# Pair attention: values projected per tile of 111 tokens, biased into a staging buffer and moved to each image's rows by DMA

## The reference

```
qkv = x @ w_attn + b_attn                     # x: 32 images x 37 tokens x 256
q, k, v = split(qkv)                          # 16 heads of 16 each
att = softmax(where(causal, q @ k.T / 4, -inf))
y = (att @ v) @ w_proj + b_proj
```

## Time and profile before

| | us |
|---|---|
| median of three executions | 1091.79 |
| the profiled execution | 1088.44 |
| its span, first to last instruction | 1086.6 |
| TensorE busy with matmuls | 905.5 (83%) |
| VectorE busy | 607.6 (56%) |
| ScalarE busy | 527.9 (49%) |
| GpSimd busy | 330.2 (30%) |
| mean granted TensorE clock | 0.898 of full |
| data moved by DMA | 47.40 MB |

### The profile page before, as it was taken

One profiled execution on the slowest core, in us unless ns is written; L12 is line 12 of the kernel. 1 busy time (PEld: TensorE's weight loads), 2 busy tenths in 40 slices (PEclk: granted clock), 3 DMA queues, 4 the chain that ended last, 5 costly groups with the idle time before them and its releaser, 6 DMA issues. The chain is left out here.

```text
span 1086.6 us, 26178 instructions
## 1 busy us (share of the span) xinstructions
PE 905.5 (83%) x10336; PEld 671.7 (62%) x10336; DVE 607.6 (56%) x1308; ACT 527.9 (49%) x942; POOL 330.2 (30%) x425
## 2 busy tenths in 40 slices
PE   6889959499999789768997299999478898998666
PEld 6778726377777557557886144444267777777424
DVE  5475656766666279754663624222554564533476
ACT  3345547566566289634452155554123333443346
POOL 1211320445553000020313324442254453532102
PEclk9999968799999899869997599999788999998885
DMA  6200030200000100001012953222220000000001
GB/s 224 83 3 2 3 117 6 82 1 3 0 0 1 45 3 1 0 8 44 20 35 77 407 173 54 42 47 48 65 86 3 2 2 2 2 3 3 1 1 45
DMA packets 24307, 47.40 MB, mean 44 GB/s; under 512 B 4720, under 2 KB 15974, under 8 KB 23555
## 3 DMA queue, kind: packets, MB, share of 16 engines
q1 hardware_dynamic: 19859, 39.09, 10.4%
q0 software_dynamic: 4336, 6.74, 3.3%
HBM read 38.35 MB, written 7.47 MB: 42 GB/s over the span
## 5 line engine op out<-in xcount | busy, mean ns | idle before, releaser
L2755 PE MATMUL psum<-L2f_EW,weights_even 128*64 x176 | 81.7, 608 | 0.5 <-ACT weights_even L2454 0.2
L2756 PE MATMUL psum<-L2f_W,weights_even 128*64 128x512 f32 x176 | 81.7, 608 | 0.0
L2415 POOL DMA_INDIRECT expert_sums<-weights_even,L2f_target x20 | 35.0, 1750 | 76.1 <-DVE weights_even L2637 56.5
L1063 PE MATMUL psum<-L_cT,weights_odd 128*128 128x222 f32 (+1 forms) x192 | 45.1, 365 | 13.2 <-DVE L_by_sin L950 11.8
L2650 DVE TENSOR_TENSOR weights_even<-psum,weights_even 128x512 f32<-128x512 f32 x22 | 15.2, 692 | 72.2 <-PE psum L2756 70.2
L2274 PE MATMUL psum<-weights_even,L1f_H 128*111 128x256 f32 x176 | 46.8, 425 | 7.5 <-DVE L1f_H L2205 7.5
L425 ACT ACTIVATE L_PT<-psum 101x296 f32<-101x296 f32 x64 | 27.0, 421 | 49.1 <-PE psum L621 49.0
L882 ACT ACTIVATE L_U<-psum 128x592 f32<-128x592 f32 x32 | 21.2, 663 | 60.4 <-PE psum L1114 60.4
L2755 PEld LDWEIGHTS psum<-L2f_EW,weights_even 128*64 128x64 f32 x176 | 22.7, 139 | 43.2 <-issue 43.2
L2462 ACT ACTIVATE L2f_W<-L2f_EW 128x1024 f32 x44 | 46.3, 1053 | 6.2 <-PE psum L2756 5.6
L366 POOL TENSOR_TENSOR L_rs<-L_mv,ln_eps 111x2 f32<-111x2 f32 (+1 forms) x12 | 3.0, 252 | 146.0 <-DVE L_mv L518 139.3
(11 more groups left out here) (462 smaller groups left out, 2621.6 us busy)
## 6 DMA issues: line engine op xcount, KB each, us to landing
L2f_EW<-experts SPq DMA_DIRECT2D x24, 512.0 KB, 13.6
weights_even<-L_w SPq DMA_DIRECT2D x4, 1024.0 KB
patch_ring<-patches SPq DMA_DIRECT2D x11, 333.0 KB, 4.7
expert_sums<-L_blank SPq DMA_DIRECT2D x1, 1184.0 KB
weights_odd<-L_wo SPq DMA_DIRECT2D x1, 1024.0 KB
expert_rows<-X SPq DMA_DIRECT2D x5, 192.0 KB
expert_sums<-X SPq DMA_DIRECT2D x5, 192.0 KB
weights_even<-tok_w SPq DMA_DIRECT2D x3, 256.0 KB, 2.9
```

What stands on the lines that cost most here:

```text
L1063: mm = nc.tensor.matmul(bank[:, h * NC2:h * NC2 + width(u)], wu[:, (2 * g + h) * 128:(2 * g + h + 1) * 128], cT[:, u % 2, n // 4, 0:width( ...
L2755: nc.tensor.matmul(core.bank(bank)[PAIR[0], :], xsT[:, j % 2, c, PAIR[0]], own, start=c == 0, stop=c == KD - 1)
L2756: mm = nc.tensor.matmul(core.bank(bank)[PAIR[1], :], xsT[:, j % 2, c, PAIR[1]], cols(W1[:, part], KD, NF)[:, c], start=c == 0, stop=c == K ...
```

## The change

Values are projected like any other dense product, one tile of 111 tokens at a time, with all 256 columns as the moving side: two matmuls a tile, four a unit, both tiles in bank M1. VectorE adds the bias for each tile into a new staging tile `by_tile`, whose rows are still the tile's (three images below one another), and whose ones are filled once. SyncE then moves each image's 37 rows to rows 0 to 36 (parity 0) and 64 to 100 (parity 1) of V: six transfers a unit, each 37 rows with one piece of 544 bytes (8 heads of 16 numbers and a one) for each of the unit's two tiles. `values` waits for these transfers in place of VectorE's addition. V has the parities apart now (2 x 8 x 17 columns for 8 x 34), so the sums come out beside each head. In L2 the copy of the blank is issued behind the first unit's transfers, and each unit's row copies behind the transfers of a later unit.

```diff
-        V = sb("V", [128, 2, IMGS, 8, 34])
+        V = sb("V", [128, 2, IMGS, 2, 8 * 17])
+        by_tile = sb("by_tile", [128, 2, 2, 2, 8 * 17])
...
+        def moves(units):
+            return 16 * sum(2 * min(PER, len(UNITS[u][2])) for u in range(units))
+
+        def rows_of(u):
+            return R if len(UNITS[u][1]) == 2 else width(u)
...
             def _(sp):
                 load_next(sp, next_loads, next_sem)
+                def move_values(u):
+                    images, n = UNITS[u][2], len(UNITS[u][1])
+                    sp.wait_ge(v_done, u + 1)
+                    after(sp, o_ps, pairs_of(u - 1))
+                    for i in range(min(PER, len(images))):
+                        for e in range(2):
+                            sp.dma_start(V[64 * e:64 * e + T, u % 2].rearrange("p (m i) e c -> p m i e c", m=2)[:, 0:n, i, e],
+                                         by_tile[i * T:(i + 1) * T, u % 2, 0:n, e]).then_inc(v_moved, 16)
...
+                sp.wait_ge(zeroed, 2)
+                move_values(0)
                 if route:
                     sp.wait_ge(blank_set, 1)
                     sp.dma_start(core.dram["expert_sums"][SUMS:SUMS + B * T, :].rearrange("(p n) d -> p n d", p=2 * T),
                                  blank[:2 * T].unsqueeze(1).broadcast_to([2 * T, B // 2, D])).then_inc(blank_out, 16)
...
+                for u in range(1, NU):
+                    move_values(u)
+                    if route and u >= 2:
+                        copy_rows(u - 2)
+                if route:
+                    copy_rows(NU - 2)
                     sp.wait_ge(blank_out, 16)
...
+                nc.gpsimd.memset(V[:], 0.0).then_inc(zeroed, 1)
...
-                nc.gpsimd.memset(V[:], 0.0)
-                pool.drain()
-                for e in range(2):
-                    last = nc.gpsimd.memset(V[64 * e:64 * e + T, :, :, :, 32 + e:33 + e], 1.0)
-                last.then_inc(zeroed, 1)
...
+                nc.vector.memset(by_tile[:], 1.0)
+                dve.drain()
...
+                def v_out(u):
+                    n, rows = len(UNITS[u][1]), rows_of(u)
+                    dve.wait_ge(v_ps, u + 1)
+                    after(dve, v_moved, moves(u - 1))
+                    for m in range(n):
+                        last = nc.vector.tensor_tensor(by_tile[:rows, u % 2, m].rearrange("p e (c d) -> p e c d", d=17)[:, :, :, 0:16],
+                                                       core.bank(M1)[:rows, m * D:(m + 1) * D].rearrange("p (e c d) -> p e c d", e=2, c=8),
+                                                       bv[:rows].rearrange("p (e c d) -> p e c d", e=2, c=8), ALU.add)
                     last.then_inc(v_done, 1)
...
+                def v_project(u):
+                    rows = rows_of(u)
+                    after(pe, k_done, u + 1 if u else 0)
+                    for m in range(len(UNITS[u][1])):
                         for kd in range(KD):
-                            for e in range(2):
-                                mm = nc.tensor.matmul(bank[64 * e:64 * e + T, i * 128:(i + 1) * 128], xT[:, u % 2, kd, at(img):at(img) + T],
-                                                      wqkv[:, kd, 2 * D + 128 * e:2 * D + 128 * (e + 1)], start=kd == 0, stop=kd == KD - 1)
+                            mm = nc.tensor.matmul(core.bank(M1)[:rows, m * D:(m + 1) * D], xT[:, u % 2, kd, m * R:m * R + rows],
+                                                  wqkv[:, kd, 2 * D:3 * D], start=kd == 0, stop=kd == KD - 1)
                     mm.then_inc(v_ps, 1)
...
                 def values(s):
                     u = s // 3
-                    pe.wait_ge(v_done, v_phases(u + 1))
+                    pe.wait_ge(v_moved, moves(u + 1))
...
-                                                      PT[:PR, s % 2, cq, b * T:(b + 1) * T], V[:PR, u % 2, (2 * s + b) % IMGS, cq, :],
+                                                      PT[:PR, s % 2, cq, b * T:(b + 1) * T],
+                                                      V[:PR, u % 2, (2 * s + b) % IMGS, :, 17 * cq:17 * (cq + 1)],
...
-                    if s == 0:
-                        v_project(0, 1)
...
-                            v_project(u + 1, 0)
+                            v_project(u + 1)
...
-                    if u + 1 < NU and s % 3 == 2 and images_of(u + 1, 1):
-                        v_project(u + 1, 1)
```

More of the change, by code:

```diff
@@ L249 @@
 PR = 64 + T
[L252 to L260, removed]
 def pairs_of(units):
@@ L390, in x_T @@
                     act.wait_ge(xT_ps, u + 1)
-                    after(act, v_ps, v_phases(u - 1))
+                    after(act, v_ps, u - 1)
                     tiles = UNITS[u][1]
@@ L491, in normalise @@
                     nc.vector.tensor_tensor(O[:PR, s % 2].rearrange("p c (e d) -> p c e d", e=2),
-                                            o[:, :, 0:32].rearrange("p c (e d) -> p c e d", e=2),
+                                            o[:, :, :, 0:16],
                                             r.unsqueeze(3).broadcast_to([PR, 8, 2, 16]), ALU.mult).then_inc(o_done, 1)
[L495 to L499, removed]
-                    for e in range(2):
[L501 to L504, removed]
+                def v_out(u):
[6 more added lines that the diff above has]
+                                                       bv[:rows].rearrange("p (e c d) -> p e c d", e=2, c=8), ALU.add)
                     last.then_inc(v_done, 1)
@@ L559, in x_T @@
                 def x_T(u):
-                    after(pe, v_done, v_phases(u, 0))
+                    after(pe, v_done, u)
                     for m, t in enumerate(UNITS[u][1]):
@@ L576, in q_project @@
                     pe.wait_ge(xT_done, u + 1)
-                    after(pe, v_done, v_phases(u))
+                    after(pe, z_done, u - 2)
                     project(u, core.bank(M2), 0, q_ps)
@@ L678, in _ @@
                 k_project(0)
-                v_project(0, 0)
-                pe.wait_ge(zeroed, 2)
+                v_project(0)
+                pe.wait_ge(zeroed, 1)
                 pe.wait_ge(set_up, 3)
@@ L3117, in layouts @@
         out[f"{n}_bqk"] = column(g[bqkv][:2 * D])
-        out[f"{n}_bv"] = np.zeros((PR, 128), np.float32)
-        for e in range(2):
-            out[f"{n}_bv"][64 * e:64 * e + T] = g[bqkv][order][2 * D + 128 * e:2 * D + 128 * (e + 1)]
+        out[f"{n}_bv"] = row(g[bqkv][order][2 * D:])
         out[f"{n}_wo"], out[f"{n}_bo"] = kmajor(wo[by_pair], KD), row(g[bo])
```

40 lines of the change are left out of this document (16 added, 24 removed).

## The result

| | before | after |
|---|---|---|
| time, median of four executions, us | 1092.48 (1082.33 to 1097.85) | 1158.49 (1149.35 to 1163.54) |
| profiled execution, us | 1088.44 | 1163.54 |
| its span, us | 1086.6 | 1161.7 |
| its mean TensorE clock, of full | 0.898 | 0.869 |
| L0's attention, us | 110.5 | 135.2 |

The account below looks back on a forecast made before the run. TensorE was taken as the bound (100.2 of 110.5 us in L2). L0's 9.6 and L2's 26.2 us plus 6 for the clock, 42 on 1088.4, gave 1131 with some distance to the median; range 1105 to 1168, its own 1118 to 1147.

Parts of the forecast that it names:

- The transfer: Six moves a unit on one DMA engine at 22 GB/s: 13.0 us from the last addition to L634's release.
- +1.6 a unit: Ordinary units of L0 and L2: the moves don't fit into 10.75 us, so the period becomes 18.05 us against 16.47.
- The clock: TensorE's slower clock after ten waits in L0 and L2: 6 us taken, with bounds of nothing and 17.
- The first units: First unit of each stage, with less room for the moves: third step's mask matmul later by 3.2 us (L0), 3.6 (L2).
- The blank: L2's second unit: its moves queue behind the blank copy of about 25 us; +21.4 us, containing the first unit's 3.6.
- TensorE's gain: Values phase in L0 and L2, one wider pass instead of two: net gain 0.7 us a unit, nothing in the last.
- the first rival: Moves of both stages spread over engines or faster, leaving only TensorE's gain and about 1.5 us a stage: 1080, chance 0.08.
- The edits costed at nothing: Both stages: fewer VectorE additions, staging and GpSimd fills, strides of 17 in L634 and the normalisation: zero each.
- The rival in which the blank doesn't hold the moves up: L2's second unit: transfers interleave or the first engine isn't shared, 16.2 us less, 1115 in all; chance 0.12.
- Moves spread over engines: Moves of both stages on two engines or more, fitting into the 10.75 us: 8 to 9 us gained, 1080; chance 0.08.
- Pieces at 14 GB/s: Moves between SBUF rows at the rate of 148 byte pieces: 6.3 us more in each of ten units, 1194; chance 0.10.

Follow-up runs that it names:

- run 1: The changed kernel with each 37-row move cut into transfers of 32 and 5 rows: 1114.06 us, ratio 1.0138 to the kernel before.
- run 11: The changed kernel with surplus matmuls in TensorE's waits for the moves, their numbers fitted to the waits: 1142.06 us, ratio 1.045 to the kernel before.
- Runs 11 and 12: Run 11 and, in the same group as yardstick, the changed kernel itself without an edit: 1142.06 and 1156.5 us, ratios 1.045 and 1.0578.
- Run 2: The changed kernel with the blank copied to DRAM from 32 rows instead of 74, same bytes and place in the queue: 1147.33 us, ratio 1.046.
- run 6: The changed kernel with L2's blank issued ahead of the first moves instead of behind them: 1164.16 us, ratio 1.0604 to the kernel before.
- run 4: The changed kernel with only 68 of the 544 bytes of each piece moved, same number of transfers and pieces: 1100.38 us, ratio 1.001.
- run 3: The changed kernel without the transfers, V filled with ones and L634 waiting for the addition alone: 1079.6 us, ratio 0.9829 to the kernel before.
- both repairs: The changed kernel with moves cut into 32 and 5 rows and the blank copied from 32 rows: 1093.98 us, ratio 0.9939 to the kernel before.

## Why the prediction was right in kind and short in size

**The transfer.** Its mechanism held in all points: one engine (share 0.06 to 0.07), 22 GB/s in its middle, and the new waits at L634. That 37 rows go to one engine follows from the rule of the Trainium skill ("DMA: Bandwidth & Descriptors", section on why a DMA increments its semaphore by 16), and run 1 agrees: cut into 32 rows and 5 rows, the same data show a share of 0.14 and let L635 run without a wait in five of the seven ordinary units. Its duration was mis-sized: 13.0 us was the term, and from the end of the additions (605.3) to the release (619.8) it is 14.5. What was too small is the data time. The rate reached the 22 GB/s taken only later: 14 and 11 GB/s in the first 2 us here, and 13 to 17 GB/s for 6 us in L0's chain that is issued from 115.71 on. In L0's chain from 93.89 on, the data move from about 95.2 to 107.8, 12.6 us for the 11.0 forecast, with 1.3 us ahead and 0.5 behind. An issue took 1.5 us and not 0.3 to 0.8, still less than the data of a move. At full clock (run 11) this alone gives units of 19.1 to 19.3 us, where the forecast had 18.05.

**The ordinary units.** The step that failed is "+1.6 a unit". Measured from third mask matmul to third mask matmul are +4.5, +2.8, +5.9 and +6.4 in L0 and +5.9, +4.7 and +6.25 in L2: 36.45 us for the 11.2 forecast. By run 11 about 20.4 of them stay at full clock (10.6 in L0 and 9.7 in L2), 9 us more than forecast, mostly the 1.5 us of each of seven transfers. 1.3 of the 9 are no fault of the transfer: the seven units took 114.0 us before, not 7 times 16.47 (the last one of each stage 15.3 and 15.1, one in L0 17.8).

**The clock.** The other 16 us are the second failed term: 6 was taken, with bounds of 0 and 17. The short waits were said to cost "a little", and they cost most. The reason is the order: a wait ends, the clock stays low behind it (0.50 for 5.5 us in the unit shown), and into this stretch falls the next unit's values pass, 3.00 us for 1.9. With it the addition and the next transfer start late, and since the transfer ends the unit, every us is passed on to the end. The units of L0 show it: behind values passes of 2.46 and 2.72 us they took 20.64 and 20.99 us, behind 3.15 and 3.64 us 21.70 and 22.34. From the unit's mask matmul to the end of its additions it was 5.94 us, against the 4.35 of the forecast. Runs 11 and 12 put 14.4 us (7 to 21) on it in the time of the kernel. The forecast's reason for a small number, that a slow stretch falls in part into the next wait, is wrong here: in the unit shown the stretch begins about 1 us before the end of its own wait and is over before the next transfer is issued, so none of it falls into the next wait. The ten waits and the 0.58 behind a gap were in the forecast; what they delay was not.

**The first units.** +5.2 us in L0 and +5.7 in L2, from the values pass to the third mask matmul, against 3.2 and 3.6. The 1.5 us of the transfer explain most of it; L634 behind the 8.4 us wait took 1.23 us for 0.77, at the slow clock, and the rest is small.

**The blank.** Forecast 21.4 - 3.6 = 17.8 us on L2's second unit, measured 36.20 - 17.95 = 18.25. Run 2 took it away, run 6 moved it to the first unit, and in run 4 it alone remained. The rival in which the blank doesn't hold the moves up is out.

**TensorE's gain.** 0.7 us a unit forecast, 0.8 measured (runs 1 and 3); and a gain of 2.0 and 1.6 us at the stages' starts (run 3) that the sum had only in the first rival (1.5 a stage). The edits costed at nothing (VectorE, the fills, the strides of 17) show no cost: the addition takes 0.41 to 0.43 us as forecast, and without the transfers both stages are shorter than before.

Added up: 10.9 (first units) + 18.25 (second unit) + 36.45 = 65.6 of the 66.0 us that the two stages grew. The forecast had 6.8 + 17.8 + 11.2 and 6 for the clock, 41.8. That 1158 still lies inside the range of 8 in 10 owes something to luck: its upper part was there for slower pieces, and it was filled by the clock and the first us of each chain. The forecast's own range ended at 1147.

**The rivals.** Moves spread over engines: false for the kernel as it is; run 3, which shows what it would be worth at best, came to 13.2 us less in the two stages, more than the rival's 8 to 9. Pieces at 14 GB/s: true only at the start of a chain (2 to 6 us), false for the rest. The time, 1158, lies between the forecast and this last rival, and it got there another way.

## What to carry to other kernels

Before a transfer is put on a path, factor its row count: 37 rows went over one engine at 22 GB/s, and as 32 + 5 rows the same bytes took 50.7 us less in the two stages; look also for other transfers with few engines on the same queue, since they stand in line on the same one. Where a wait of TensorE comes just ahead of work that starts the next transfer, price the slow clock in full in each period (here 2 us of each 21), because what it delays is the next wait's end. And price a saving together with what it needs: 0.8 us of TensorE a unit was bought with a 14.5 us transfer in a gap of 10.75, and with both repairs 0.6% is left of what the rest of the change is worth without transfers (1.7%, interval 0.9 to 2.5).

## What the hardware showed that was not expected

- A chain of moves from SBUF to SBUF over one engine ran slower at its start (14 and 11 GB/s in the first 2 us of one, 13 to 17 GB/s for 6 us in another) and at 22 GB/s later, with the engine's share the same.
- An issue on SyncE took 1.5 us where the moves go over one engine (six in 9.3 us), 0.75 where they are split (12 in 9.0 us), and 0.67 over one engine with an eighth of the bytes (six in 4.03 us).
- Moves from GpSimd's queue used about three engines at a time but carried 32 GB/s in all, with 1.35 us of GpSimd for each issue.
- Behind waits of TensorE of 3 to 5 us, one in each 21 us, the clock is granted at 0.50 (from about 597 to 603.7 us around the wait that ends at 598.22); three surplus matmuls in the wait kept it at 1.00.
